# Cross-attention and a routed feed-forward layer on one core: GpSimd's queue issues the query diagonals, SyncE keeps those of the keys

## What is computed

```python
x = x + xattn(layernorm(x), ctx, ctx, mask)      # 16 heads, head dim 8, softmax over 128 keys
h = layernorm(x)                                 # 2048 tokens
probs = softmax(h @ wg.T); top 2 of 8, weights normalised to sum 1
y = einsum('tei,ehi->teh', silu(h @ w1) * (h @ w3), w2)
x = x + einsum('te,teh->th', expert_w, y)
```

## Time and profile before

| | |
|---|---|
| median of 3 runs | 327.0 us (326.06 to 329.75) |
| profiled execution, its own time | 327.09 us |
| its span | 325.3 us |
| TensorE (PE) busy | 233.3 us, 72% |
| VectorE (DVE) busy | 219.9 us, 68% |
| ScalarE (ACT) busy | 141.8 us, 44% |
| GpSimd (POOL) busy | 114.3 us, 35% |
| mean granted TensorE clock | 0.871 of full |

### The profile page before, as it was taken

The page is one execution under the profiler, slowest core; times in us unless marked ns, Lnnn a source line. Parts: engine busy times, 40 slices in busy tenths (PEclk is TensorE's granted clock), DMA queues, the critical chain, the costliest instruction groups (busy, mean ns, idle before and its releaser), DMA issues.

```text
span 325.3 us, 5807 instructions
## 1 busy us (share of the span) xinstructions
PE 233.3 (72%) x1591; PEld 180.4 (55%) x1591; DVE 219.9 (68%) x642; ACT 141.8 (44%) x318; POOL 114.3 (35%) x125
## 2 busy tenths in 40 slices
PE   0946788889898988747564818679674698899820
PEld 0733565667566656546342606658563697789710
DVE  5597965887598758857734424387862586688983
ACT  6792256546655664206321406335220354455400
POOL 5201250125011502033737360035277264555540
PEclk9986599999999999957977566799985699999975
DMA  6995504450443044510301154102113134428006
GB/s 177 256 260 105 123 2 87 83 115 11 90 91 81 2 97 99 134 61 2 82 24 53 34 111 97 27 8 61 50 51 70 33 82 94 106 51 217 26 11 194
DMA packets 43886, 27.31 MB, mean 84 GB/s; under 512 B 5030, under 2 KB 41397, under 8 KB 43856
## 3 DMA queue, kind: packets, MB, share of 16 engines
q1 hardware_dynamic: 40208, 20.95, 28.2%
q0 software_dynamic: 2816, 5.27, 5.4%
q10 hardware_dynamic: 832, 0.72, 0.8%
HBM read 13.27 MB, written 7.37 MB: 63 GB/s over the span
## 4 chain that ended last, share of the span: by engine, by line
PE 41%; DVE 20%; issue 9%; another core or an unknown queue 8%; SPq 7%; DMA 7%; ACT 5%; POOL 2%; POOLq 0%; DVEq 0%; ACTq 0%
PE bank L493 6%; SPq L421 6%; PE bank L499 4%; DVE m_neg L1356 4%; DMA bd<-st 3%; PE bank L649 3%; PE bank L731 3%; PE bank L652 2%; PE bank L666 2%; PE bank L732 2%; PE bank L705 2%; PE bank L718 2%; PE bank L627 2%; PE bank L708 2%
## 5 line engine op out<-in xcount | busy, mean ns | idle before, releaser
L1016 POOL DMA_INDIRECT ys<-big x46 | 45.3, 986 | 41.5 <-DVE big L1379 22.6
L1356 DVE TENSOR_REDUCE m_neg<-bank 128x4 f32<-128x512 f32 x64 | 43.4, 685 | 18.1 <-PE bank L666 17.8
L905 ACT ACTIVATE big<-bank 128x512 f32<-128x512 f32 x64 | 37.5, 597 | 25.6 <-PE bank L652 24.0
L774 ACT ACTIVATE st<-bank 128x128 fp32r<-128x128 f32 (+1 forms) x92 | 26.3, 329 | 35.0 <-PE bank L718 12.9
L731 PE MATMUL bank<-bd,st 128*128 x92 | 28.1, 327 | 10.5 <-DVE big L1379 10.1
L649 PE MATMUL bank<-m_bd,ones_b 128*128 128x512 f32 x64 | 31.7, 496 | 3.7 <-ACT big L905 1.9
L666 PE MATMUL bank<-bd,st 128*128 128x512 f32 x64 | 29.1, 477 | 7.2 <-DMA bd<-st 5.8
L968 POOL TENSOR_SCALAR ve<-mv 128x4 f32<-128x4 f32 x8 | 1.8, 228 | 87.0 <-DVE mv L1048 87.0
L1398 DVE TENSOR_TENSOR big<-big,bank 128x256 f32<-128x256 f32 x46 | 19.3, 419 | 16.2 <-ACT big L937 13.6
L1283 DVE SCALAR_TENSOR_TENSOR st<-st_hi,cst,bank 128x512 fp32r<-128x512 f32 x32 | 23.3, 747 | 8.8 <-ACT st_hi L774 4.3
L937 ACT ACTIVATE big<-bank 128x256 f32<-128x256 f32 x46 | 17.7, 385 | 25.9 <-PE bank L708 13.1
(11 more groups left out here) (172 smaller groups left out, 566.4 us busy)
## 6 DMA issues: line engine op xcount, KB each, us to landing
bd<-st SPq DMA_DIRECT2D x128, 64.0 KB, 2.1
big<-xg SPq DMA_DIRECT2D x46, 64.5 KB
raw<-ys SPq DMA_DIRECT2D x8, 256.0 KB, 3.2
xg<-in_patterns SPq DMA_DIRECT2D x18, 64.5 KB
x_all<-in_x SPq DMA_DIRECT2D x4, 256.0 KB, 4.3
rows<-in_mask_BxS_if POOLq DMA_DIRECT2D x4, 256.0 KB, 5.0
ctx_all<-in_L_ffn_w SPq DMA_DIRECT2D x1, 1024.0 KB, 5.9
out<-ctx_all SPq DMA_DIRECT2D x4, 256.0 KB, 3.8
```

Of the source, the lines that this page charges most:

```text
L774: return nc.scalar.activation(o, i, ACT.Copy)
L905: nc.scalar.activation(prob[n % 2][:, NJ * g:NJ * (g + 1), :].rearrange("p h q -> p (h q)"), s2[k % 2][:, :], ACT.Exp, scale=SCALE).then_i ...
L1016: pool.indirect_dma_start(ys[f], bass.IndirectOffsetOnAxis(xt[n % XR][:, D:RW].bitcast(I32), 0), y_sb[n % YR], None, bounds_check=2 * CAPS ...
L1356: nc.vector.tensor_reduce(m_neg[:, H * (b - 1) + NJ * g:H * (b - 1) + NJ * (g + 1)], s1[k % s1_ring(u)][:, :].rearrange("p (j q) -> p j q" ...
```

## The change

The function of the query diagonals moves from SyncE's program to GpSimd's, with the same waits and four transfers each. SyncE's order becomes keys 4u to 4u+3 of each pass. On GpSimd the queries stand between its other work: in pass 0 queries 0, 1, 2 after ck and the mask load; in pass u from 1 to 3 query 4u-1 after m_bd, 4u and 4u+1 after ve/rstd, 4u+2 after ck and the mask load; in pass 4 query 15 after m_bd and ahead of ve/rstd number 6. In pass 3 `inverse_deviation(4)` comes ahead of queries 12 and 13, `inverse_deviation(5)` behind them.

```diff
@@ sync
-            def block_diagonal(k, n):
+            def key_diagonal(n):
                 u, b = divmod(n, QB)
-                stacks_in(sp, u, k)
+                stacks_in(sp, u, 1)
                 if n >= 3:
-                    sp.wait_ge(s1_full if k else s2_full, NG * (n - 2))
+                    sp.wait_ge(s1_full, NG * (n - 2))
...
-                for k, b in ((1, 0), (1, 1), (1, 2), (0, 3), (1, 3)):
-                    if k and u < NQ:
-                        block_diagonal(1, QB * u + b)
-                    if not k and u >= 1:
-                        block_diagonal(0, QB * (u - 1) + b)
                 if u < NQ:
-                    block_diagonal(0, QB * u)
-                    block_diagonal(0, QB * u + 1)
-                    block_diagonal(0, QB * u + 2)
+                    for b in range(QB):
+                        key_diagonal(QB * u + b)
@@ gpsimd
+            def query_diagonal(n):
+                u, b = divmod(n, QB)
+                stacks_in(pool, u, 0)
+                if n >= 3:
+                    pool.wait_ge(s2_full, NG * (n - 2))
+                else:
+                    pool.wait_ge(bd_cleared, 6)
+                for j in range(NJ):
+                    rows = slice(R * j, R * (j + 1))
+                    pool.dma_start(bd_slot(0, n)[rows, :, j, :].bitcast(F32), st[rows, u % 2, 0, :, b * S:(b + 1) * S].bitcast(F32)
+                                   ).then_inc(qbd_ready[n % 3], 16)
...
                         nc.gpsimd.tensor_tensor(m_bd[:, NJ * g:NJ * (g + 1), :], ...).then_inc(mbd_ready, 1)
+                    query_diagonal(QB * u - 1)
                 if u + 1 < NQ:
                     inverse_deviation(u + 1)
+                if u + 1 == NQ:
+                    inverse_deviation(NQ)
+                if 1 <= u < NQ:
+                    query_diagonal(QB * u)
+                    query_diagonal(QB * u + 1)
+                if u + 1 < NQ:
                     mask_context(u + 1)
                     if u + 2 < NQ:
                         load_mask(u + 2)
                 if u + 1 == NQ:
-                    inverse_deviation(NQ)
                     inverse_deviation(NQ + 1)
+                if u == 0:
+                    query_diagonal(0)
+                    query_diagonal(1)
+                if u < NQ:
+                    query_diagonal(QB * u + 2)
```

More of the change, by code:

```diff
@@ L408, in _ @@
                              w.rearrange("e (c p) h -> p (e c) h", p=P)).then_inc(in_w13, 16)
-            def block_diagonal(k, n):
+            def key_diagonal(n):
                 u, b = divmod(n, QB)
-                stacks_in(sp, u, k)
+                stacks_in(sp, u, 1)
                 if n >= 3:
-                    sp.wait_ge(s1_full if k else s2_full, NG * (n - 2))
+                    sp.wait_ge(s1_full, NG * (n - 2))
                 else:
-                    sp.wait_ge(bd_cleared, 3 if k else 6)
+                    sp.wait_ge(bd_cleared, 3)
                 for j in range(NJ):
                     rows = slice(R * j, R * (j + 1))
-                    sp.dma_start(bd_slot(k, n)[rows, :, j, :].bitcast(F32), st[rows, u % 2, k, :, b * S:(b + 1) * S].bitcast(F32)
-                                 ).then_inc((kbd_ready if k else qbd_ready)[n % 3], 16)
+                    sp.dma_start(bd_slot(1, n)[rows, :, j, :].bitcast(F32), st[rows, u % 2, 1, :, b * S:(b + 1) * S].bitcast(F32)
+                                 ).then_inc(kbd_ready[n % 3], 16)
             for u in range(NQ + 1):
```

## The result

The kernel after takes 336.35 us (median of 4 runs, 335.12 to 339.73), the kernel before beside it 326.99 us: ratio 1.029 (95% interval 1.021 to 1.037). Slower, as forecast, but by 9.4 us where 4.9 were forecast. The profiled execution took 335.12 us, its span is 333.3 us: 8.0 us over that of before.

A forecast was written before the change was run, and what follows sets the result against it. The prediction took SyncE's diagonals to cost only 1.05 us on the path, and a VectorE stall in pass 4 to stall the kernel. 327.09 - 1.05 + 6.0 = 332.0 us, range 329 to 341.

The forecast's parts named there:

- The chain is no price list: SyncE's diagonal copies: the inferred chain's 6% at line 421 is not a gain; only 1.05 us is on the path.
- rival E: Passes 1 to 3: SyncE's queue really held them, so the kernel gets faster, 313 us outermost or about 323; chance 0.04.
- Price of a copy, 0.65 us: GpSimd's queue: issuing one direct diagonal copy takes 0.65 us, at the far end 1.28; four make 2.6 us.
- B: GpSimd's queue: copies are dear, toward 1.28 us each, costing pass 0 and pass 4 more; 336 to 340.6 us; chance 0.15.
- C: Any burst on GpSimd, not only scatters, brings a standstill: 344 us, at most 349; chance 0.12.
- Pass 0 hidden: Pass 0: twelve query copies ahead of m_bd cost nothing; m_bd ends at 49.5, 1.5 us before TensorE's last need.
- Gain of 1.05 us: Before the first scores of batch 3: TensorE's wait at 62.48 for query diagonal 3 goes, saving 1.05 us.
- Pass 4: Last attention pass: query 15's copies wait for their slot and hold ve/rstd, VectorE and the scatters; 6.0 us charged.
- 6.0: Pass 4: the scatter bursts start 6.0 us late, and this delay was charged in full to the kernel.
- 4.6: Pass 4: VectorE, at line 1065 from 154.60, stands 4.6 us for rstd, delaying TensorE's transpose equally.
- Rival D: Pass 4: the delay is taken up later and only part of 4.6 us arrives, 326 to 330.3 us; chance 0.19.
- The expert stage: Stage after the first load of sorted rows: no term in the sum, so a change of 0 us.

The follow-up runs named there:

- the variant on SyncE alone: Kernel before with SyncE issuing query diagonal 3 (7, 11) behind two keys, not three: 304.01 against 304.75 us (ratio 0.996), then 305.28 against 305.20 (0.9975).
- query 15 on SyncE: Kernel after with only query diagonal 15 (four copies) given back to SyncE: 304.94 against 304.61, 306.71 against 304.75, 305.76 against 305.20 us for the kernel before.
- query 15 alone: Kernel before with only query diagonal 15 (four copies) moved to GpSimd, ahead of reciprocal deviation number 6: 310.55 against 305.20 us, ratio 1.0146.

## Why the prediction was right or wrong

**The chain is no price list: right.** The 6% at line 421 became nothing, and rival E (faster) fell.

**Price of a copy, 0.65 us: too high, harmless.** Line 983 shows 548 ns at the least and in the median, 622 at the worst; the nearest rows for it were the mask loads, not the scatters. It is 53 ns under SyncE's own 601. The forecast's ground, a count of pieces like that of both, isn't borne out by the profile's count of packets: 32 for a copy on GpSimd's queue ((4864 - 2816) / 64), 144 for one on SyncE's ((40208 - 30992) / 64).

By the port rule of the Trainium skill ("SBUF — State Buffer", "SBUF: two separate sides") GpSimd's transfers starve while certain VectorE instructions hold the port. The issue times, 64 of 64 within 74 ns beside a working VectorE, show nothing of it. The landings have a median of 2.2 us as SyncE's keys have 2.1, but a worst of 6.3 against 3.9; whether that one late copy is such a case no run here shows.

B falls by the price, C by the waits of passes 0 to 3: behind bursts of 12 and 8 copies the profile names no unassigned wait of any engine.

**Pass 0 hidden: right.** m_bd ends at 48.55; forecast were 49.5 at most.

**Gain of 1.05 us: right at its place, two thirds of it left at pass 4, and hard to see.** The wait at 62.48 went. In the absolute starts of m_bd little shows: 73.83 in place of 74.24 in pass 2, 143.18 in place of 143.21 in pass 4. The kernel before has there:

```profile
74.24 4.40 POOL L989 TENSOR_TENSOR m_bd<-mT,cst 128x512 fp32r<-128x512 f32 x4 [4.01 <-DVE mT L1256]
...
143.21 4.03 POOL L989 TENSOR_TENSOR m_bd<-mT,cst 128x512 fp32r<-128x512 f32 x4 [13.04 <-DVE mT L1256]
```

But the trace of the kernel after was 0.65 us behind before the change could act: its mask load of pass 0 starts at 37.35, that of the kernel before at 36.70, and no query copy is issued until then. Counted from this load, m_bd of pass 2 comes 1.06 us earlier (36.48 in place of 37.54), m_bd of pass 4 0.68 earlier (105.83 in place of 106.51). In all traces the stretch from that load to m_bd of pass 4 is 106.2 to 107.9 us in the five with all queries in SyncE's old order up to there, 105.5 to 107.2 in the seven with them on GpSimd; the means differ by 0.7. The spread is as large as the difference, so the gain's size isn't settled, and the variant on SyncE alone gives no more than a hint of one (0.7 us faster, then 0.1 slower).

**Pass 4: mechanism right, its 6.0 met by luck.** The stall of VectorE was 4.73 (forecast 4.6), the shift of the first load from the start of m_bd 6.42 (forecast 6.0). Two terms under the 6.0 were off, however. The slot came free 1.9 us later after the start of m_bd (13.76 us: 156.94 - 143.18; before 11.87: 155.08 - 143.21); the sum had put this at nothing. And the four copies took 2.19 in place of 2.6. With both put right the delay of the burst, the forecast's choice, is 7.5, and the scatters do start 7.39 late (160.71 - 153.32); the delay by the stall is 6.1 in place of 4.6, and VectorE's line does start 5.95 late (160.55 - 154.60). The first load moved 6.4, nearer to the second.

That stretch up to the copies had 0.59 of the clock, and in the later traces too its length goes with the clock: 11.1 us at 0.81 (155.86 - 144.77, kernel after), 12.2 at 0.71 (156.34 - 144.16, before), 13.7 at 0.59 (155.72 - 142.02, after), 14.0 at 0.59 (157.18 - 143.23, query 15 alone). The rest have 13.2 to 13.3 with query 15 on SyncE, 13.3 and 12.2 where only SyncE's order changes. It falls either way for the kernel after, so these traces don't tie it to the change; they don't rule out a part of it either.

**Choosing 6.0 over 4.6: not borne out.** From the copies on, the price was 4.5 us with the standstills and 4.3 without (table above), near the stall and not the burst's delay. Rival D described this as "only part of the 4.6 us arrives"; it is the burst's delay that is partly taken up, VectorE's stall is not. The prediction's 6.0 came out close because the slot's 1.9 us, which it did not have, stand in for what it charged the burst too much.

**The expert stage: 0 in the sum, 1.6 us in the trace.** So the profiled difference adds up as 0.65 (the later start) - 0.68 + 6.42 + 1.6 = 8.0 us (335.12 - 327.09 = 8.03). The forecast had -1.05 + 6.0 + 0; of its three terms this one was the most mis-sized. In this stage, too, ScalarE has unassigned waits in both kernels; those of the kernel after, from who waited for whom,

```profile
ACT big L930 <- remote: 6.1, 1, 6.1
...
ACT st L767 <- remote: 4.3, 2, 3.9
```

stand against 6.0 us in two waits of line 937 (930 now) before, the longest 4.0. VectorE had one of 3.5 us before and has one of 1.4 now. That these make the 1.6 us is argued, not shown. In the later traces the stage takes 112.1 to 115.9 us, in no order with the edits (113.0 and 115.0 in the kernel after, 112.7 and 115.9 where only SyncE's order changes), so 1.6 us lies within what it varies by itself. The last 1.3 us of the 9.4 is how the medians lie to the profiled executions (336.35 and 326.99 against 335.12 and 327.09). Of the 8.0 us, 2.3 (the start and the expert stage) and the slot's 1.9 are tied by nothing here to the change; what the later runs show for it is 4 to 5 us, which the forecast's total of 4.9 meets too.

## What to carry to other kernels

Before a waiting transfer is moved to another engine's queue, list what is queued behind it there and how much slack its users have; one wait of 9.7 us with 1.5 us of slack behind it outweighed sixty free copies. The share of a queue in an inferred chain is not a gain. A removed wait of TensorE may be one, but look for it from a common point ahead of the change: absolute starts hid 0.7 us here behind a start that was 0.65 later. And when a term comes out close, put the measured pieces into it: here a 6.0 that met 6.4 hid a wrong choice. If such a transfer must go to the busy engine, put what others wait for ahead of it: rstd first made the same move cost 0.9 us on the medians instead of 4.2 to 4.6.

## What the runs showed of the hardware

The same program took 327 us in one measurement and 300 to 308 in all later ones. The mean clock doesn't separate them (0.871 in the slower profiled execution, 0.869 to 0.913 in the later ones of that kernel). In pass 4 the difference is standstills of 3 to 9 us that end 1.5 to 1.8 us behind a burst of indirect scatters; 16.8 us more lie in the expert stage. One more trace of theirs: in the summary of the transfers neither the scatters nor the loads of sorted rows of the slower measurement have a time to landing, and in the faster they have 2.4 and 1.9 us:

```profile
xg<-rows,rows_i POOLq DMA_INDIRECT x24, 2.4
```

What caused both is open. A forecast of 1 to 2% that rests on such a standstill holds for the measurement that it was read from.

A direct copy of 64 KB between tiles costs GpSimd 0.55 us of issue and lands 2.2 us later, in 32 packets; from SyncE it is 0.60 and 2.1 us, in 144 packets.
